# Interaction-network tower: unit loads that read x1 in SBUF, and row gathers released by products

## What is computed

```python
def _cin_forward(X0, Ws):
    F_ = X0.shape[1]
    Xk = X0
    outs = []
    for W in Ws:
        H_prev = Xk.shape[1]
        Wr = W.reshape(F_, H_prev, W.shape[1])
        Xk = jnp.einsum('bfd,bhd,fho->bod', X0, Xk, Wr)
        outs.append(Xk.sum(axis=2))
    return jnp.concatenate(outs, axis=1)
...
h = jnp.concatenate([z, dense_ctx], axis=1)
h = jnp.maximum(h @ W_top1 + b_top1, 0.0)
h = jnp.maximum(h @ W_top2 + b_top2, 0.0)
y = h @ W_top3
```

## Time and profile before

| | |
|---|---|
| median of 3 runs | 585.45 us (584.02 to 591.72) |
| the profiled execution's own time | 578.03 us |
| its span, first to last instruction | 576.2 us |
| PE busy | 370.3 us (64%) |
| DVE busy | 307.3 us (53%), 192 + 48 products among it |
| ACT busy | 137.1 us (24%) |
| POOL busy | 187.3 us (33%), 192 gathers |
| DMA moved | 64.30 MB, mean 112 GB/s |
| mean granted TensorE clock | 0.911 |

### The profile page before, as it was taken

The page is one execution under the profiler, slowest core; times in us unless marked ns, Lnnn a source line. Parts: engine busy times, 40 slices in busy tenths (PEclk is TensorE's granted clock), DMA queues, the critical chain, the costliest instruction groups (busy, mean ns, idle before and its releaser), DMA issues.

```text
span 576.2 us, 7709 instructions
## 1 busy us (share of the span) xinstructions
PE 370.3 (64%) x3000; PEld 168.8 (29%) x3000; DVE 307.3 (53%) x305; ACT 137.1 (24%) x282; POOL 187.3 (33%) x196
## 2 busy tenths in 40 slices
PE   0010200856088439726998269755999998999995
PEld 0010000212022115302452025212553553553554
DVE  1010001473278347643789348526799798798930
ACT  1000000001022113302333123303253353251253
POOL 6777773027506720672017700771000000000000
PEclk9999999977779759976999869777999999999999
DMA  6000100191436326721757246702756847848300
GB/s 163 6 7 7 7 7 4 41 252 29 98 107 150 86 60 190 211 57 40 190 165 188 45 123 186 197 7 63 227 160 173 222 139 195 221 140 208 90 1 1
DMA packets 28039, 64.30 MB, mean 112 GB/s; under 512 B 7311, under 2 KB 10823, under 8 KB 28012
## 3 DMA queue, kind: packets, MB, share of 16 engines
q1 hardware_dynamic: 21868, 62.35, 40.3%
q0 software_dynamic: 6144, 1.59, 3.0%
HBM read 53.86 MB, written 5.85 MB: 104 GB/s over the span
## 4 chain that ended last, share of the span: by engine, by line
another core or an unknown queue 33%; PE 24%; DMA 14%; DVE 11%; issue 8%; ACT 4%; POOL 4%; SPq 2%; DVEq 0%; ACTq 0%
PE acc L622 14%; DVE pairs L416 8%; DMA units<-x_dram 5%; DMA turned<-x_dram 5%; POOL emb L388 4%; PE spread L596 2%; DMA x_dram<-common 2%; PE misc L683 1%; ACT x0diag L489 1%; DVE z L421 1%; SPq L328 1%; ACT x0parts L476 1%; DVE rest L284 1%; DMA units<-x 1%
## 5 line engine op out<-in xcount | busy, mean ns | idle before, releaser
L416 DVE TENSOR_TENSOR pairs<-spread,units 128x1024 f32<-128x1024 f32 x192 | 225.9, 1218 | 118.3 <-remote 76.4
L388 POOL DMA_INDIRECT emb<-in_tbl,ids_sb x192 | 187.1, 975 | 203.2 <-DVE parts L288 143.6
L622 PE MATMUL acc<-pairs,w_sb 128*64 128x512 f32 x768 | 205.2, 642 | 4.4 <-DVE pairs L416 4.3
L596 PE MATMUL spread<-x0parts,sel 72*64 72x512 bf16 (+1 forms) x280 | 50.6, 450 | 116.9 <-ACT common L476 39.6
L622 PEld LDWEIGHTS acc<-pairs,w_sb 128*64 128x64 f32 x768 | 53.3, 146 | 76.0 <-issue 54.3
L416 DVE TENSOR_TENSOR pairs<-turned,common 120x1024 f32<-120x1024 f32 x42 | 51.1, 1220 | 24.6 <-DMA turned<-x_dram 24.6
L596 PEld LDWEIGHTS spread<-x0parts,sel 72*64 72x64 bf16 (+1 forms) x280 | 14.6, 121 | 159.3 <-ACT common L476 71.4
L643 PE MATMUL misc<-ident_b,parts 128*72 128x128 bf16 x120 | 11.7, 253 | 67.0 <-DVE parts L288 36.9
L622 PE MATMUL acc<-pairs,w 120*64 120x512 f32 x180 | 49.6, 636 | 2.4 <-DVE z L421 2.1
L416 DVE TENSOR_TENSOR pairs<-spread,common 120x1024 f32<-120x1024 f32 x6 | 7.3, 1223 | 68.9 <-remote 65.1
L476 ACT ACTIVATE x<-acc 128x512 f32<-128x512 f32 x31 | 18.7, 602 | 96.8 <-PE acc L622 80.2
(11 more groups left out here) (57 smaller groups left out, 192.6 us busy)
## 6 DMA issues: line engine op xcount, KB each, us to landing
units<-x_dram SPq DMA_DIRECT2D x56, 512.0 KB, 6.2
turned<-x_dram SPq DMA_DIRECT2D x42, 480.0 KB
units<-x SPq DMA_DIRECT2D x16, 256.0 KB, 5.1
x_dram<-x SPq DMA_DIRECT2D x28, 128.0 KB
emb<-in_tbl,ids_sb POOLq DMA_INDIRECT x192
x_dram<-common SPq DMA_DIRECT2D x14, 96.0 KB
x_dram<-common SPq DMA_DIRECT2D x14, 56.0 KB
w_sb<-in_w SPq DMA_DIRECT2D x2, 384.0 KB
```

Of the source, the lines that this page charges most:

```text
L388: pool.indirect_dma_start(out=e3[:, f, :], out_offset=None, in_=tables[f], in_offset=bass.IndirectOffsetOnAxis(ap=ids_sb[:, t, f:f + 1], a ...
L416: dve.tensor_tensor(pairs[buf][0:rows, :], source[0:rows, :], other[0:rows, h * HALF:(h + 1) * HALF], ALU.mult).then_inc(pairs_done, 1)
L596: last = pe.matmul(spread[ring][lo:hi, half * BLK:(half + 1) * BLK], sel[:, first + lo:first + hi], src[:, cols(h, half)], start=True, sto ...
L622: last = pe.matmul(acc[half * H:(half + 1) * H, :], w, pairs[buf][0:rows, half * BLK:(half + 1) * BLK], start=first, stop=final)
```

## The change

Three things are edited.

**Units.** The round trip of x1 through HBM is gone for all tiles: `store_x1`, `x1_dram`, `x1_stored` and ACT's wait on it (`x1_read`) are removed, and `load_units(t, h)` does for every tile what `first_units` did for tile 0: 8 DMAs of 256 KB per half, read from `x1` in SBUF, waiting for `x1_done` and, from tile 2 on, for the products that read the buffer last.

**SP's order.** The written-out order becomes a plain loop: for each tile both halves of `store_x0` and `load_turned`, then both halves of `load_units`. The loads of the h = 1 units are no longer interleaved with the next tile's stores.

**Gathers.** For tiles 3 to 7, each of the 24 gathers waits for one more product of DVE. Gather f of tile t waits for product number 21 + (7f)//6 counted from the start of step t-3: the first behind product 21 of that step, the last (f = 23, 21 + 26 = 47) behind product 17 of step t-2, three products ahead of the split that reads it. The wait for the buffer stays.

```diff
+GATHER_FROM = 21
...
-            def store_x1(t, h):
+            def load_units(t, h):
 
                 sp.wait_ge(x1_done, 2 * t + h + 1)
-                for half in range(2):
-                    sp.dma_start(x1_dram[h][:, half * BLK:(half + 1) * BLK], x1[half * H:(half + 1) * H, h, :])\
-                        .then_inc(x1_stored, 16)
-
-            def load_units(t, h, js):
-
-                sp.wait_ge(x1_stored, 64 * (t - 1) + 32 * (h + 1))
-                for j in js:
+                for j in range(UNIT_GROUPS):
                     if t >= 2:
 
                         last = MIDDLE.items.index(("L2", FIELD_GROUPS - 1, j, h))
                         sp.wait_ge(pairs_done, item(t - 2, last) + 1)
-                    rows = x1_dram[h][j:H:UNIT_GROUPS, :].rearrange("v (u c) -> v u c", u=1)
-                    sp.dma_start(units[t % 2][:, j, h * HALF:(h + 1) * HALF], rows.to_broadcast([UNITS, FIELDS, HALF]))\
-                        .then_inc(units_in[t % 2][h][j], 16)
...
                     for half in range(2):
                         rows = x1[half * H + j:(half + 1) * H:UNIT_GROUPS, h, :].rearrange("v (u c) -> v u c", u=1)
-                        sp.dma_start(units[0][:, j, h * HALF + half * BLK:h * HALF + (half + 1) * BLK],
-                                     rows.to_broadcast([UNITS, FIELDS, BLK])).then_inc(units_in[0][h][j], 16)
+                        sp.dma_start(units[t % 2][:, j, h * HALF + half * BLK:h * HALF + (half + 1) * BLK],
+                                     rows.to_broadcast([UNITS, FIELDS, BLK])).then_inc(units_in[t % 2][h][j], 16)
...
-            for h in range(2):
-                first_units(h)
-            store_x0(1, 0)
-            load_turned(1, 0, range(L1_CHUNKS))
+            load_units(0, 0)
+            load_units(0, 1)
             for t in range(1, TILES):
-
-                store_x0(t, 1)
...
+                for h in range(2):
+                    store_x0(t, h)
+                    load_turned(t, h, range(L1_CHUNKS))
+                for h in range(2):
+                    load_units(t, h)
...
                 for f in range(F):
+                    if t >= 3:
+
+                        pool.wait_ge(pairs_done, item(t - 3, GATHER_FROM + f * 7 // 6) + 1)
                     pool.indirect_dma_start(
...
-                        dve.wait_ge(units_in[slot][h][j], (i - slot) * 8 + 16 * (2 - slot))
+                        dve.wait_ge(units_in[slot][h][j], (i - slot) * 16 + 32)
...
             def take_x1(last_item, tile, h, bank):
 
-                x1_read(act, tile, h)
```

More of the change, by code:

```diff
@@ L184, in build_tower @@
         x0_dram = [nc.dram_tensor(f"x0_dram{h}", (X0_ROWS, HALF), F32).ap() for h in range(2)]
-        x1_dram = [nc.dram_tensor(f"x1_dram{h}", (H, HALF), F32).ap() for h in range(2)]
         spread = [ctx.enter_context(nc.psum_tensor(f"spread{s}", [P, HALF], F32)) for s in range(2)]
@@ L207, in build_tower @@
         turned_in = [sem(f"turned_in{c}") for c in range(L1_CHUNKS)]
-        x1_stored = sem("x1_stored")
         units_in = [[[sem(f"units_in{s}_{h}_{j}") for j in range(UNIT_GROUPS)] for h in range(2)] for s in range(2)]
@@ L317, in load_units @@
                         sp.wait_ge(pairs_done, item(t - 2, last) + 1)
-                    rows = x1_dram[h][j:H:UNIT_GROUPS, :].rearrange("v (u c) -> v u c", u=1)
-                    sp.dma_start(units[t % 2][:, j, h * HALF:(h + 1) * HALF], rows.to_broadcast([UNITS, FIELDS, HALF]))\
-                        .then_inc(units_in[t % 2][h][j], 16)
-            def first_units(h):
-                sp.wait_ge(x1_done, h + 1)
-                for j in range(UNIT_GROUPS):
                     for half in range(2):
                         rows = x1[half * H + j:(half + 1) * H:UNIT_GROUPS, h, :].rearrange("v (u c) -> v u c", u=1)
-                        sp.dma_start(units[0][:, j, h * HALF + half * BLK:h * HALF + (half + 1) * BLK],
-                                     rows.to_broadcast([UNITS, FIELDS, BLK])).then_inc(units_in[0][h][j], 16)
+                        sp.dma_start(units[t % 2][:, j, h * HALF + half * BLK:h * HALF + (half + 1) * BLK],
+                                     rows.to_broadcast([UNITS, FIELDS, BLK])).then_inc(units_in[t % 2][h][j], 16)
             def store_x0(t, h):
@@ L350, in load_turned @@
                     sp.dma_start(turned[c][:, :], bass.AP(rows.tensor, rows.offset, steps)).then_inc(turned_in[c], 16)
-            for h in range(2):
-                first_units(h)
-            store_x0(1, 0)
-            load_turned(1, 0, range(L1_CHUNKS))
+            load_units(0, 0)
+            load_units(0, 1)
             for t in range(1, TILES):
-                store_x0(t, 1)
-                load_turned(t, 1, range(L1_CHUNKS))
-                store_x1(t, 0)
-                load_units(t, 0, range(UNIT_GROUPS))
-                store_x1(t, 1)
-                if t < TILES - 1:
-                    load_units(t, 1, (0,))
-                    store_x0(t + 1, 0)
-                    load_units(t, 1, (1,))
-                    load_turned(t + 1, 0, (0, 1))
-                    load_units(t, 1, (2,))
-                    load_turned(t + 1, 0, (2,))
-                    load_units(t, 1, (3,))
-                else:
-                    load_units(t, 1, range(UNIT_GROUPS))
+                for h in range(2):
[3 more added lines that the diff above has]
+                    load_units(t, h)
             sp.wait_ge(misc_free, rounds(TILES - 1) + len(SIDE_LAST) + len(TAIL))
@@ L526, in take_common @@
                 copy(common[:, h * HALF:(h + 1) * HALF], spread[buf][0:COMMON_ROWS, :]).then_inc(common_done, 1)
-            def x1_read(eng, tile, h):
-                if isinstance(tile, int) and tile == 1:
-                    for j in range(UNIT_GROUPS):
-                        eng.wait_ge(units_in[0][h][j], 32)
-                elif not isinstance(tile, int) or tile > 1:
-                    eng.wait_ge(x1_stored, 64 * (tile - 2) + 32 * (h + 1))
             def take_x1(last_item, tile, h, bank):
-                x1_read(act, tile, h)
                 act.wait_ge(main_done, last_item + 1)
```

## The result

The changed kernel takes 515.67 us (median of 4 runs, 513.68 to 517.02) where the kernel before takes 584.74 on the same chip (583.07 to 591.72). The ratio is 0.884, 95% interval 0.880 to 0.888: faster by 69 us. The forecast was 480 with a range of 458 to 527.

What follows compares the result with a forecast made beforehand. A resource taking 1.40 to 1.44 us per gather, fed every 1.25, was taken to hold PE's signals. Start 125.2, steps 298.0 and tail 47.3 gave 470.5; 1.8 and 7.4 more made 479.7, forecast 480 us, range 458 to 527.

Steps and rivals of the forecast that it cites:

- The mechanism: POOL issues gathers every 1.25 us, a resource takes 1.40 to 1.44 each; the growing backlog holds up PE's signals.
- rival B: Gathers in steps 1 to 5 still felt, a small backlog holding signals, 10 us per step: 527 us; chance 16%.
- Start, 125.2 us: Stretch up to the first mark: gathers of tiles 0 to 2 keep order and waits, change 0.
- Units, 2 us per step: Unit loads from SBUF go out at once after x1: 2 us gained per step, quiet step 41.5.
- Step 0 and step 6, the tail: Stretches outside steps 1 to 5: step 0 at 44 us, step 6 without gathers 41.5, tail 47.3.
- Gathers, 1 us per step: Steps 1 to 5: gathers spread over products use 91% of the resource, costing 1 us per step; steps of 42.5.
- The brake: Gathers behind products: if PE's signals are held, products stop, then gathers stop, so the scheme brakes itself.
- rival D: Gathers in flight, not their backlog, hold signals: five steps of 81 us, 672 us; decided from 63.7 per step; chance 4%.
- Split and last gather, 0 to 4 us (rival C): Split may wait 0 to 4 us for its last gather; rival: 4 unhidden in five steps, 500 us, chance 10%.
- The port: SBUF port shared by POOL's gathers and DVE's products with both inputs in SBUF: costed at 0 for DVE.
- rival E: The stalls are not POOL's and move elsewhere; only the units' 2 us in seven steps are won: 571; chance 5%.
- The 7.4 us carried over: The earlier median's 7.4 us above its profiled execution, added to 472.3 to give 479.7.

Runs made afterwards that it cites:

- e10: The kernel of e7 with a 128 x 256 fill on POOL behind each gather of tiles 3 to 7: 479.53 us, ratio 0.812.
- e12: The kernel of e11 with gather f of tile 2 also waiting for DVE's product (5f)//6: 463.33 us, ratio 0.784.
- e11: The kernel of e10 with the fills starting at tile 2 instead of tile 3: 476.71 us, ratio 0.821.
- e5: The changed kernel, unedited, measured again where no signals were held: 434.42 us for 431.36 before.
- e2: The changed kernel without the gathers' waits on products, signals not held: 418.22 us, ratio 0.979.
- e9: The changed kernel without the gathers' waits on products, same edit as e2, signals not held: 417.75 us, ratio 0.968.
- e3: The kernel before with only the gathers' waits on products added, signals not held: 442.71 us, ratio 1.031.
- e7: The changed kernel with gather f released behind product 10 + (5f)//4 instead of 21 + (7f)//6, signals held: 503.08 us, ratio 0.867.

## Why the prediction was right, and where it was not

**The mechanism.** Right in the main for the case it was read from: gathers issued close together hold PE's signals (e10), and a resource that takes 1.43 us per gather says when the long holds end (the reckoning above). The number is fitted and the resource is inferred. e12's start came out by it. e10's steps (44 to 49 us for 42 to 44) and e12's time did not, and e11's mark only in part. The forecast was written without knowing that there is a case in which nothing is held. That the change was measured in the case it was read from was luck: in the other it gains nothing (e5).

**The signs that it had named.** By its own test, wrong if steps 1 to 5 exceed 46 us, the forecast of the steps failed: they are 48.4 to 54.9, with a granted clock of 0.94 to 1.00 for the 1.00 named, and "remote" is 16.9 us for under 15. The start (124.1), the unit loads within 1 us of x1 (407.82 to 407.85), DVE's wait for units (4.5 us in all) and the quiet step came as named. The time lies in the range because the range reached as far as rival B, not because the forecast's sum held.

**Start, 125.2 us.** 124.1: right. e12 shows that 28 us of it (124.1 to 95.7) come with tile 2's gathers being issued ahead of the first products, which the forecast had taken as fixed.

**Units, 2 us per step.** Right as far as it was seen: the quiet step is 41.2 for 43.5, and the kernel without the release gains 13 to 15 us over seven steps (e2, e9) where nothing is held. In the steps with held signals the units' part was never measured alone. That the h = 1 loads stand ahead of the next tile's store cost nothing to be seen: four waits for `turned` of 4.4 us together.

**Step 0 and step 6, the tail.** 42.7, 41.2 and 48.2 for 44, 41.5 and 47.3: within 1.3 us.

**Gathers, 1 us per step.** This is the step that failed. Steps 1 to 5 were forecast as 42.5 and came out at 51.6 on average: 45.7 us in five steps, against 43.8 by which the span of 470.5 missed the 514.3. The rest cancels (start -1.1, step 0 -1.3, step 6 -0.3, tail +0.9). The size is rival B's, 10 us per step, which I had given 16%. The sum had set the mean use, 91%, and in a burst a backlog of 0.6 us. Both numbers leave out two things. A held signal does not wait for the 0.6 us, it waits until gathers issued after it are served too (3.7 to 3.8 us in the rows from 313.77, where two of the four started after the spread had ended). And the gathers do not keep the products' distance: they come in runs at 1.25 us (the four from 316.11). The row that I had leaned on, eight products in 9.13 us without a wait, shows that DVE has stock for the start of a set; it does not show a step's loss, since there the following 12.41 us are the bill. Against the quiet step the truth, 10 us, lies midway between the two rows that it had named as nearest, 0 and 20 us; taking 1 was a choice without a measurement.

**The brake.** The traces fit one: DVE's longest wait for a late signal fell from 12.4 to 4.8 us, POOL stood while DVE stood (319.85 to 323.69), and rival D's 63.7 us per step was never near. It limits a hold and does not prevent one. No run takes the brake away and leaves the mean distance, so its share is argued and not shown.

**Split and last gather, 0 to 4 us (rival C).** In the measured case one wait of 2.3 us. Where nothing is held it is what the change costs: five waits of 3.6 to 5.3 us, and with them the whole of the units' gain (e5, e3). I had the price per step right, 4 us, and not that it depends on DVE's pace: a held DVE gives the gathers time to land, as the single wait here against the five of e5 suggests.

**The port.** A gather beside a product with both inputs in SBUF took 1.84 us instead of 0.94 (the row from 313.96), the product beside it (from 313.77) its usual 1.22: the cost of 0 for DVE stands. The Trainium skill ("SBUF — State Buffer", section "SBUF: two separate sides") has the first to start win for a whole instruction; here all the waiting seen was POOL's. A product with both inputs in SBUF that began at 310.37, inside the gather of 310.09 to 311.03, was not held up and took 1.22 us too. The sentence of the same section of the Trainium skill that a DMA and a compute operation cannot slow each other would have made rival E likeliest; e7 and e10, which differ in nothing but the fills that space the gathers, stand 18 us apart in steps 1 to 5, so here the measurement decides against it, as far as the time between PE's end and its signal's arrival is concerned.

**The 7.4 us carried over.** They did not appear: the median of the changed kernel, 515.67, is 0.5 below its profiled execution. It made the miss 36 us and not 44.

**What stays open.** What decides whether signals are held in a measurement. It is no matter of the kernel, since the kernel before does both, and one of the chips showed not held, held and not held in three measurements, one after the other; nothing was tried on it. Neither part of the change was measured alone in the held case (e2, e3 and e9 were not held), so how the 69 us divide between units, SP's order and release is argued from steps; SP's order was never taken apart from the units. Which resource it is that takes 1.43 us is not seen in any row, nor what still holds signals when gathers are 1.54 us apart. That the wide window cures the late rows where nothing is held was not tried either (e7 ran held), nor was e2 in the held case: its expectation of 570 is an estimate without a measurement. And why steps 1 and 2 of e12 are 4 us longer than the later ones was not followed.

## What to carry to other kernels

When an engine starts long after its input was ready and the profile says "remote", look at what else runs in all such waits and divide its time by its count: 1.43 us per gather against an issue of 1.25 was enough to say when the long holds end, though not how long a step becomes. Spread such work by its own distance and not only by a count of someone else's work, since a wait for a count that has been passed lets everything through at once; and a mean use under 100% says nothing about a signal that comes in the middle of a burst. Time the kernel before beside every version, in more than one measurement: the change is worth 12% in one condition of the chip and nothing in the other.

## What the runs showed of the hardware that was not expected

The same program takes 431 to 433 us in three measurements and 578 to 585 in five. In the first, ACT copies `common` 1.1 us after the spread's start with 1.25 us between gathers (e9), in the second 10.1 us after it, and the second copy 21.3 us after it. No clock explains it: step 6 of the changed kernel, without gathers, has a granted clock of 1.00 in both, and takes 41.2 us held and 41.0 not held (e5).

How long ACT is held at the start does not follow from the backlog's size. The wait is 10.18 us twice in the kernel before, twice in e11 and once in e12 (67.59), with gathers 1.25 us apart ahead of it or, for the second of e11, 1.55. The reckoning says when the last hold ends, not how many there are or how long one lasts.

POOL's own signal to itself is held as well. In e11 the wait for a fill that has ended is 0.27 us as a rule, and 0.8 to 1.4 four times between 82 and 92 us, in the start's backlog:

```profile
83.74 0.95 POOL L365 DMA_INDIRECT emb<-in_tbl,ids_sb  x1 [1.39 <-POOL filler L371]
...
92.14 0.95 POOL L365 DMA_INDIRECT emb<-in_tbl,ids_sb  x1 [1.37 <-POOL filler L371]
```
